# Early-fusion block on one core: the end of the first attention stage re-ordered, and one maxima product per head placed ahead of the value products

## The reference, cut to what matters

```
h = concatenate([edges(x), txt], axis=1)                 # 8 x 384 x 256
h = h + attention0(layernorm(h))                         # 16 heads of 16, two softmaxes (K and K'), mixed by alpha
h = h + ffn0(layernorm(h))                               # both operands of each product in blockwise FP4

def fp4_quant_dequant(x):                                # blocks of 16 along the last dim
    scale = max(max|block| / 6, 1e-12)
    q = nearest grid value of |x / scale| * sign * scale # grid 0, .5, 1, 1.5, 2, 3, 4, 6
def fp4_linear(x, w): return einsum(quant(x), quant(w))
ffn0 = fp4_linear(silu(fp4_linear(x, w_gate)) * fp4_linear(x, w_up), w_down)
```

## Time and profile before

| | us |
|---|---|
| median of 3 runs | 1869.66 (1868.59 to 1869.83) |
| the profiled execution, its own time | 1862.18 |
| span of the profiled execution, first to last instruction | 1860.4 |
| PE busy in the span | 1757.0 (94%) |
| DVE, ACT, POOL busy | 1007.1, 674.2, 407.2 |
| mean granted clock of PE | 0.982 |

### The profile page before, as it was taken

The page is one execution under the profiler, slowest core; times in us unless marked ns, Lnnn a source line. Parts: engine busy times, 40 slices in busy tenths (PEclk is TensorE's granted clock), DMA queues, the critical chain, the costliest instruction groups (busy, mean ns, idle before and its releaser), DMA issues. The chain is left out here.

```text
span 1860.4 us, 29106 instructions
## 1 busy us (share of the span) xinstructions
PE 1757.0 (94%) x9935; PEld 1118.6 (60%) x9935; DVE 1007.1 (54%) x2072; ACT 674.2 (36%) x1289; POOL 407.2 (22%) x415
## 2 busy tenths in 40 slices
PE   7989999899999987899989999997999999999997
PEld 3324444344444433677755656655676768999997
DVE  6597877778777877788874554442311111122221
ACT  2116655556566675455432332223111110111110
POOL 2101021120211001788831212110121211100100
PEclk9989999999999999999999999998999999999999
DMA  6832632525425111000056000000010003343311
GB/s 198 132 54 65 91 78 40 99 53 84 78 40 93 25 48 56 17 0 0 1 198 195 1 0 0 0 0 1 18 37 23 30 24 102 124 151 102 105 32 33
DMA packets 111955, 112.84 MB, mean 61 GB/s; under 512 B 11455, under 2 KB 104433, under 8 KB 111858
## 3 DMA queue, kind: packets, MB, share of 16 engines
q1 hardware_dynamic: 98610, 83.21, 20.1%
q10 hardware_dynamic: 9600, 18.92, 2.9%
q0 software_dynamic: 3648, 9.46, 1.4%
HBM read 78.51 MB, written 32.93 MB: 60 GB/s over the span
## 5 line engine op out<-in xcount | busy, mean ns | idle before, releaser
L925 DVE TENSOR_REDUCE mx<-ps_a 128x1 f32<-128x384 f32 x768 | 383.2, 550 | 66.3 <-PE ps_a L567 63.8
L789 ACT ACTIVATE prob<-ps_a 128x768 f32<-128x768 f32 (+1 forms) x512 | 306.2, 650 | 118.7 <-PE ps_a L580 118.6
L567 PE MATMUL ps_a<-w,qs 96*128 96x384 bf16 x768 | 220.1, 338 | 12.3 <-DVE mx L925 5.2
L580 PE MATMUL ps_a<-qs,w 100*128 100x384 bf16 x768 | 208.8, 332 | 6.1 <-issue 3.4
L2090 PEld LDWEIGHTS ps_e<-xTr,w 128*128 128x128 f32 x1792 | 206.1, 193 | 2.2 <-issue 0.8
L2090 PE MATMUL ps_e<-xTr,w 128*128 128x128 f32 x1792 | 206.3, 276 | 0.6 <-DVE xTr L2263 0.6
L567 PEld LDWEIGHTS ps_a<-w,qs 96*128 96x128 bf16 x768 | 61.4, 98 | 180.8 <-DVE mx L925 116.6
L2026 PE MATMUL ps_e<-xT_all,w 128*128 (+1 forms) x512 | 169.3, 490 | 0.9 <-ACT xT_all L2117 0.9
L591 PE MATMUL ps_a<-prob,vp 128*32 128x384 f32 x1536 | 164.1, 500 | 0.0
L2026 PEld LDWEIGHTS ps_e<-xT_all,w 128*128 128x128 f32 x512 | 97.4, 192 | 66.2 <-issue 1.4
L2153 ACT ACTIVATE gel_r<-ps_e 128x512 f32<-128x512 f32 x56 | 33.4, 597 | 280.9 <-PE ps_e L2090 280.9
(11 more groups left out here) (253 smaller groups left out, 2490.2 us busy)
## 6 DMA issues: line engine op xcount, KB each, us to landing
w<-parts_dram SPq DMA_DIRECT2D x192, 96.0 KB, 5.3
w<-in_L_ffn_W_dram ACTq DMA_DIRECT2D x18, 1024.0 KB, 8.3
parts_dram<-w SPq DMA_DIRECT2D x24, 576.0 KB, 3.4
qs<-parts_dram SPq DMA_DIRECT2D x96, 96.0 KB, 4.0
prob<-in_x_dram SPq DMA_DIRECT2D x24, 256.0 KB, 3.6
w<-in_L_ffn_W_dram SPq DMA_DIRECT2D x6, 1024.0 KB, 12.6
grouped_x<-empty_row SPq DMA_DIRECT2D x1, 4352.0 KB, 23.7
grouped_h<-empty_row SPq DMA_DIRECT2D x1, 4240.5 KB, 33.1
```

The lines of the kernel that those rows point to most:

```text
L567: mm = pe.matmul(ps[:, r % 3, 0:T], qs[0:NS, b, u // 2, t * P:(t + 1) * P], ks[0:NS, b, u % 2, u // 2], start=True, stop=True)
L580: mm = pe.matmul(ps[:, 4 + t, 0:T], ks[0:NS + 4, b, kp, hh, t * P:(t + 1) * P], qs[0:NS + 4, b, hh], start=True, stop=True)
L789: act.activation(prob[:, g % 2, j, ts.start:ts.stop], ps[:, 4 + ts.start:4 + ts.stop, 0:T], ACT.Exp).then_inc(exp_done.sem, 1)
L925: dve.tensor_reduce(at, ps[:, r % 3, 0:T], AX.X, ALU.max).then_inc(ring_free.sem, 1)
```

## The change

It has two parts.

1. Ring order. In a unit with a next image, the second ring entry moves from behind the value products to in front of them.
2. The last turn and the stage's end.
   - The weights' DMAs no longer wait for the zeroes but only for the scores of the image before; the zeroes cover only what the DMAs don't write; the three matrices have a semaphore each, and the first three quarters each wait for their own.
   - The 36 rounding steps are spread over units 5 to 29, and the aggregation of seven images' moments moves from unit 28 to unit 24.
   - Turning the weights waits by matrix, for two, three and four quarters, and is cut into pieces of 2, 3, 2 and 2 groups with the finishing of the last image between them. Turning y and the output projection use banks 3 and 7 alternately.
   - All three tiles of image 0 are quantised at the end of the stage on DVE, ACT and POOL, tile 0 alone is turned there. `middle` starts with no input to quantise, and its pipeline skips tile 2 too.
   - The roots of the last image move from ACT's end of the stage to the start of `middle`; the roots of the others move in front of the copy of the last outputs.

```
-                sp.wait_ge(w4_zero.sem, 3)
+                sp.wait_ge(st_done.sem, st_done.at(B - 1, 0))
...
                         scores(i, b, v, 1)
+                        if more:
+                            ring(i + 1, 1 - b, ring_part(v)[1:2])
                         if j and g:
                             values(i, b, g - 1, j - 1)
...
-                            ring(i + 1, 1 - b, ring_part(v)[1:])
+                            ring(i + 1, 1 - b, ring_part(v)[2:])
...
+                        if n % SETS == 0:
+                            pe.wait_ge(w4_step.sem, w4_step.at(n // SETS + 2, 0))
...
-                pe.wait_ge(w4_step.sem, w4_step.at(4, 0))
-                turn_feed_forward_weights(0, len(TURN_BANKS))
-                last = in_bank3("turn_outputs", i, GROUPS - 1, last)
-                turn_feed_forward_weights(len(TURN_BANKS), len(moves) // 4)
+                turn_feed_forward_weights(0, 2)
+                in_bank3("turn_outputs", i, GROUPS - 1, last)
+                turn_feed_forward_weights(2, 5)
+                pe.wait_ge(y_done.sem, y_done.at(i, GROUPS))
                 for k in range(KC):
-                    last = in_bank3("turn_y", i, k, last)
-                last = in_bank3("output", i, 0, last)
+                    turn_y(i, k, (3, 7)[k])
+                turn_feed_forward_weights(5, 7)
+                output(i, 0)
+                turn_feed_forward_weights(7, len(moves) // 4)
+                output(i, 1, 7)
...
                 feed_forward_roots(0, B - 1)
-                copy_feed_forward_weights(0, len(TURN_BANKS))
+                copy_outputs(B - 1, GROUPS - 1)
+                copy_feed_forward_weights(0, 5)
                 copy_y(B - 1, 0)
-                copy_feed_forward_weights(len(TURN_BANKS), len(moves) // 4)
-                copy_y(B - 1, 1)
+                copy_y(B - 1, 1, 7)
+                size_first(0)
+                copy_feed_forward_weights(5, 7)
+                size_first(1)
+                copy_feed_forward_weights(7, len(moves) // 4)
+                size_first(2)
                 act.wait_ge(first_turned.sem, 1)
                 act.copy(F.xT[:, 0].rearrange("p k t -> p (k t)"), ps[:, 4, 0:C]).then_inc(first_copied.sem, 1)
-                feed_forward_roots(B - 1, B)
...
-                    n, units = 4 * w4_step.per, UNITS - 9
-                    return range(n * (v - 7) // units, n * (v - 6) // units) if 7 <= v < 7 + units else ()
+                    n, units = 4 * w4_step.per, UNITS - 7
+                    return range(n * (v - 5) // units, n * (v - 4) // units) if 5 <= v < 5 + units else ()
...
+                    if n < 3 and k == 0:
+                        dve.wait_ge(w4_in[n].sem, 16 if n == 2 else 32)
...
-                        if v == UNITS - 4 and not more:
+                        if v == UNITS - 8 and not more:
                             gather_moments(0, B - 1)
...
+                for t in range(TT):
+                    quantize_first(t)
+                add(B - 1, 0)
+                new_moments(B - 1, range(2))
+                add(B - 1, 1, 7)
+                new_moments(B - 1, range(2, TT))
                 gather_moments(B - 1, B)
...
-                        if present(t, 2, False, last):
+                        if present(t, 2, False, last) and not (first and t == 0):
...
-                size_inputs(0, 1)
+                act.activation(rstd[:, NT - TT:], mv[:, NT - TT:, 1], ACT.Sqrt, bias=G["eps"][:]).then_inc(last_root.sem, 1)
```

More of the change, by code:

```diff
@@ L296, in attention0 @@
         dn4 = w4[:, 2 * NGU:].rearrange("p (a n) -> p a n", n=PAD0)
-        w4_in, w4_zero, w4_step, _ = sig("w_fp4_in"), sig("wzero"), sig("wstep", 9), None
+        w4_in = [sig(f"w_fp4_in{n}") for n in range(3)]
+        w4_zero, w4_step = sig("wzero"), sig("wstep", 9)
         F = FeedForwardTiles(E)
@@ L601, in turn_outputs, with turn_y, output @@
                     mm.then_inc(oT_done.sem, 1)
-                def turn_y(i, k):
+                def turn_y(i, k, bank=3):
                     pe.wait_ge(ys_done.sem, ys_done.at(i, GROUPS // 2))
                     for t in range(TT):
-                        mm = pe.transpose(ps[:, 3, t * P:(t + 1) * P], y[:, t, k * P:(k + 1) * P], ident[:])
+                        mm = pe.transpose(ps[:, bank, t * P:(t + 1) * P], y[:, t, k * P:(k + 1) * P], ident[:])
                     mm.then_inc(yt_done.sem, 1)
-                def output(i, n):
+                def output(i, n, bank=3):
                     pe.wait_ge(yT_done.sem, yT_done.at(i, KC))
@@ L745, in _ @@
                 mm.then_inc(first_turned.sem, 1)
-                last = in_bank3("output", i, 1, last)
             @block.scalar
@@ L953, in normalize, with add @@
                                              ).then_inc(y_done.sem, 1)
-                def add(i, n):
+                def add(i, n, bank=3):
                     dve.wait_ge(op_done.sem, op_done.at(i, n + 1))
@@ L959, in add, with new_moments @@
                     at = h[:, bass.ds(i * TT + 2 * n, t)]
-                    dve.tensor_tensor(at, at, ps[:, 3, 0:t * C].rearrange("p (t c) -> p t c", t=t), ALU.add
+                    dve.tensor_tensor(at, at, ps[:, bank, 0:t * C].rearrange("p (t c) -> p t c", t=t), ALU.add
                                       ).then_inc(h_done.sem, 1)
-                def new_moments(i):
-                    dve.wait_ge(h_done.sem, h_done.at(i, 2))
-                    for t in range(TT):
+                def new_moments(i, tiles=range(TT)):
+                    dve.wait_ge(h_done.sem, h_done.at(i, 2 if TT - 1 in tiles else 1))
+                    for t in tiles:
                         dve.bn_stats(bn[:, i * TT + t], h[:, i * TT + t]).then_inc(hs_done.sem, 1)
@@ L1520, in turn @@
                     for t in range(TT):
-                        if present(t, 2, False, last):
+                        if present(t, 2, False, last) and not (first and t == 0):
                             inputs(*tile_at(i, t, 2))
                         hidden(i, t, first)
-                pool.sem_inc(xp_step.sem, 2)
-                pool.sem_inc(xq_done.sem, 1)
-                inputs(0, 1)
+                pool.sem_inc(xp_step.sem, 2 * TT)
+                pool.sem_inc(xq_done.sem, TT)
                 for_images(pool, turn)
```

88 lines of the change are left out of this document (45 added, 43 removed).

## The result

The changed kernel takes **1853.55 us** (median of 6 runs, 1850.21 to 1856.26) against 1869.12 us for the kernel before in six runs beside it: ratio 0.9927, 95% interval 0.9912 to 0.9942. The kernel before had medians of 1866.32, 1866.63 and 1864.31 us in three later sets of 11 to 27 runs, so the 1869.66 us that the forecast started from was high. In those sets the gain is about 11.8 us. The forecast was 1860.6 us (1857.0 to 1865.7), with a gain of 9.1 us.

The account below looks back on a forecast made before the run. PE, busy 94% of the span, bounds the kernel, so only its idle time counts: 4.2 us from the ring order plus 4.9 from the last turn and stage's end, 9.1 off 1869.66, gives 1860.6 us (1857.0 to 1865.7).

Parts of the forecast that it names:

- the base: Starting time 1869.66 us: profiled execution 1862.18, with the 7.5 us difference to the other runs' median carried unchanged.
- everywhere else in these units PE is not held: In the turns, away from the transposes' waits for DVE, PE isn't held, so an earlier product gains nothing there.
- the 14.47 us of the stage's end: Before the change, the chain from the last rounding step to the stage's last instruction, 718.14 to 732.61.
- The transposes: Transposes of the maxima in units 15 and 31 start 0.2 to 0.38 us earlier, 4.2 us in all.
- I price it at nothing: A bank wait in front of the value products, tightest at a turn's start, was taken to cost nothing.
- the rival on the slower side: Moved product waits for its bank in 7 x 24 units; at 0.08 us each, 1874.0 us; chance 0.07.
- The last turn: DVE's first rounding step in the last turn starts 4.4 us earlier, and the last one ends 3.2 us earlier.
- The stage's end: Last rounding step to the stage's last instruction, on POOL, takes 12.8 instead of 14.5 us; stage ends 4.9 us earlier.
- the 0.8 for collisions: At the stage's end, DVE's quantising beside POOL is slowed: 0.8 us added on the longest path.
- up to 1.0 us more: First eight products of `middle`, behind longer PE idle time: up to 1.0 us more or 1.5 less, taken as 0.
- the long wait: PE's 4.73 us wait in `middle` hangs on quantising the hidden tile and tile 3 behind it; it stays unchanged.

Follow-up runs that it names:

- part 1 alone: The kernel before with only the ring order of the change, second ring entry in front of the value products: 1859.47 us, ratio 0.9965.
- the kernel with one wait: The changed kernel, but the first rounding step waits for the DMAs of all three matrices as before the change: 1855.46 us, ratio 0.9952.
- before again: The kernel before, run and profiled once more without an edit: 1866.18 us, ratio 0.9999.
- half rings: The kernel before, second ring entry in front of the values only in units 15 and 31, or only in all others: 1863.69 and 1864.67 us.

## Why the prediction was right and wrong

The time lies 7.1 us below the 1860.6 forecast. Of that, 3.3 us is the base: 1869.66 us was too high. 2.7 us is the gain, 11.8 instead of 9.1, and two steps sized it wrong: "everywhere else in these units PE is not held" (part 1 took 6.8 us off the turns instead of 4.2), and the 14.47 us of the stage's end, which came from one execution at the higher clock level. Since the gains read from the profiles add up to more than the timed 11.8, how the 2.7 divides between the two isn't settled. The last 1.0 us is that the first six runs of after lay low.

**Part 1, mechanism right, incomplete.** Forecast 4.2 us, measured 6.8 in the first pair of profiles, 6.9 in the time of part 1 alone. The intervals of the transposes give 2.6 us for the seven ahead of unit 15 and 4.3 for the seven ahead of unit 31. Three terms were wrong (turns counted from 0):
- *The transposes*: 7 x 0.30 + 7 x 0.26 = 3.9 us instead of 4.2. From the last product's end to the transpose it takes 0.65 us, where I had 0.57 (516.63 to 517.20).
- *"Everywhere else in these units PE is not held"* failed. Units 24 and 28 had a wait inside a merged row: 0.46 us a turn, 3.2 in seven. Units 8 and 20 of turn 0 and unit 12 of turn 6 fall by 0.23 us each too, which makes 3.9. The view of waits didn't list these; the rows' durations did.
- *"I price it at nothing"* failed too, the other way: 0.14 us each in unit 1 of turns 1, 2 and 4 and in unit 23 of turns 1 to 6, and 0.08 in unit 18 of turn 6, which makes 1.3 us. The slack of 0.05 us at the turn's start was read from where the value products began, 0.26 us behind the last score product; a ring product that isn't held starts 0.17 behind it, so there was none. The view behind the earlier trace rows also has a row for it, in before (total, times, longest):

```profile
PE ps_a L567 <- DVE mx L925: 5.0, 6, 1.9
```

Three of these six come ahead of the first turn. The other three are waits of 0.49 to 0.61 us for a bank in unit 1 of turns 1, 2 and 4, just ahead of the place where the moved product went. In unit 23 DVE is late behind an addition (L977, 498.18 us) and three moments (L984, 1.08 us from 498.75). That is the rival on the slower side, in 2 of 24 units.

These make 3.9 + 3.9 - 1.3 = 6.5 us. The other 177 units change by 0.03 us or less each and grow by 0.5 in all. Another 1.0 us is the start of turn 5, whose interval was 39.84 us in before and 38.64 after: PE ran at the lower level for a part of it before (windows of PE, before at 519 us and after at 518 us; columns as above),

```profile
519.00:523.00 4.00, 4.00 (x20) 0.57 0.06 10
```

```profile
518.00:522.00 4.00, 3.73 (x25) 1.00 0.04 8
```

and in no profile with a changed ring order, while all three with the old one have it. Around PE's long wait for issue, ahead of turn 3, two differences cancel: the wait is 0.66 us longer after, the unit behind it 0.59 shorter. The sum is 6.5 - 0.5 + 1.0 - 0.1 = 6.9, against 6.8 measured.

**The last turn, right.** The first step was to come 4.4 us earlier (measured 4.5) and the last 3.2 (measured 3.5); between the second profiles it is 3.8 and 3.0. That DVE hands its lateness on without a further pause is shown by the kernel with one wait: of 4.1 us at the first step 3.0 are left at step 4 and 2.9 at the last.

**The stage's end, the chain right, the base wrong.** 12.8 us came out to the hundredth and POOL ends the stage, though the 0.8 for collisions is made up otherwise than forecast. But the 14.47 us that I subtracted from were those of one execution in which PE kept 2.4 GHz. In the four other profiles with the old end (before again, part 1 alone, the two half rings) the 24 transposes took 4.17 to 5.36 us, the stage ended 16.1 to 17.3 us behind the last rounding step, and the last transpose of maxima lies 76.2 to 78.0 us ahead of `middle`, not 74.7. With the new end PE doesn't idle over 1.2 us there, and it kept 2.4 GHz in all nine profiles. The stage's end alone is thus 1.7 us shorter against the profile shown and 3.3 to 4.5 against the others. From the last transpose to `middle` the saving is 5.5 us against the profile shown and 7.0 to 8.7 against the others, two of which (the half rings) also have a stretch at the lower level in the last turn. The Trainium skill (TensorE: Matmul & The Clock Gate, Part 1) states that an idle array falls to the lower level and that the number of matmuls that then run slow varies from run to run of one kernel; the two profiles of before, 2.81 and 4.17 us behind the same 3.0 us of idle time, agree.

**middle, right with a shift of the clock.** I took 0 of "up to 1.0 us more": the first eight products took 5.0 instead of 4.08 us, and the stretch to the last `gate_up` grew by 0.2. The 4.08 was that one execution's too: in the four other profiles with the old end the same eight took 3.99 to 5.01 us. That the long wait hangs on image 1's first tile is shown by the kernel that quantises it later. What I hadn't asked is whether three tiles at the stage's end are the right number. One is better by 4.3 us: tiles 1 and 2 lengthened the only chain at the end and `middle` didn't need them so early.

**The base, wrong.** I carried a 7.5 us difference between the profiled execution and the median of three runs, as if both were fixed. The typical time of before is some 1866.4 us, 3.3 less than the three runs that I had. With the 2.7 us more of gain and the 1.0 of the low runs, that is the whole distance from 1860.6 to 1853.55.

## What to carry to other kernels

A merged row that takes longer than its count times the usual duration hides a wait: compare durations of the same group along the loop before writing that an engine isn't held. The slack in front of a moved instruction is counted from where that instruction could start, not from where the one that stood there did. Before a stall of DVE is priced at its own length, ask what PE's clock does behind the idle time it makes; here that was worth another 1.7 to 2.9 us. And when work is moved out of a busy start, move only what the start really waits for: of three tiles quantised early, two cost 4.3 us. And a base of three runs is not enough where the runs of one kernel spread over 7 to 10 us.

## What the runs showed of the hardware

- Identical code differs between executions by as much as these edits are worth: the stretch ahead of the first transpose took 106.5 to 111.6 us in fourteen profiles, and runs of one kernel spread over up to 10 us (before, 1862.71 to 1872.37). That spread goes with the mean granted clock. The changed kernel's six runs took 1850.21 us at 0.985, 1852.24 at 0.984, 1853.5 and 1853.6 at 0.983, 1856.0 and 1856.26 at 0.981: about 1.5 us for each 0.001.
- Behind the same idle time of 3.2 to 3.3 us, eight products of `middle` took 2.60 us in two profiles and 4.01 in another.
- In the rows of the stage's end every quantising step of DVE with two inputs in SBUF that begins beside an instruction of POOL from 716.58 us on ends a fixed time behind POOL's end, so a short one suffers most. L1172 (128x16) takes 0.17 us at 716.40, where POOL is idle, and 0.70 at 718.95, ending 0.03 us behind POOL; the steps of 128x256 end 0.28 us behind it. Reductions and reciprocals beside POOL keep their 0.42 and 0.25 us.
